# Folding attention's high and low sums by plain turns and a pair sum on VectorE, and a new order of the recurrence's work among the experts

## The reference, cut to what matters

```
x: 4 x 1024 x 512
# layer 0
xn = layernorm(x)
attn: per head h of 8: two score maps softmax(q_i k_i^T, causal), i = 1, 2 (dh 64)
      a = map_1 - map_2 * lambda;  o = a @ v_h           # 1024 x 64 per head
      o = o * rsqrt(mean of squares in groups of 8 + 1e-6) * (1 - l_init);  out = o @ Wo
ffn:  (silu(xn W1) * (xn W3)) -> Hadamard transform -> W2
x = x + attn(xn) + ffn(xn)
# layer 1
xn = layernorm(x)
rec:  f = sigmoid(xn Wf), c = silu(xn Wc), r = silu(xn Wr)
      h_t = f_t h_(t-1) + (1 - f_t) c_t  along the 1024 rows of a batch
      rec = (r * rmsnorm(h)) @ Wo
moe:  router over 64 experts, 8 per token, at most 128 tokens an expert
      expert: (silu(xb Wg) * (xb Wu)) @ Wd, scaled by the gate, added to its tokens
x = x + rec(xn) + moe(xn)
```

## Time and profile before

| what | value |
|---|---|
| median of three runs | 3428.03 us |
| profiled execution | 3419.29 us, span 3417.1 us, clock 0.968 |
| PE busy | 3156.6 us (92%) |
| PEld busy | 2458.4 us (72%) |
| DVE busy | 1780.5 us (52%) |
| ACT busy | 1258.1 us (37%) |
| POOL busy | 1610.9 us (47%) |

### The profile page before, as it was taken

The page is one execution under the profiler, slowest core; times in us unless marked ns, Lnnn a source line. Parts: engine busy times, 40 slices in busy tenths (PEclk is TensorE's granted clock), DMA queues, the critical chain, the costliest instruction groups (busy, mean ns, idle before and its releaser), DMA issues. The chain is left out here.

```text
span 3417.1 us, 45950 instructions
## 1 busy us (share of the span) xinstructions
PE 3156.6 (92%) x16426; PEld 2458.4 (72%) x16426; DVE 1780.5 (52%) x3865; ACT 1258.1 (37%) x2829; POOL 1610.9 (47%) x1410
## 2 busy tenths in 40 slices
PE   5999999899999989999998999999968799998996
PEld 3778787777778777877777787787736567676764
DVE  5455556655555555555566656555536453424431
ACT  3344444434434343443334344333333222332322
POOL 2356657634554653364455336445522334443442
PEclk8999999999999999999999999999979899999998
DMA  7432323353222234211122421112064568685867
GB/s 214 155 117 99 105 90 105 118 176 111 81 90 93 93 114 151 97 65 69 62 81 96 151 98 64 68 62 74 29 218 155 150 169 234 183 221 167 212 182 151
DMA packets 219392, 424.78 MB, mean 124 GB/s; under 512 B 22432, under 2 KB 103072, under 8 KB 217120
## 3 DMA queue, kind: packets, MB, share of 16 engines
q1 hardware_dynamic: 200608, 377.79, 32.9%
q0 software_dynamic: 18560, 44.05, 7.0%
HBM read 311.09 MB, written 110.69 MB: 123 GB/s over the span
## 5 line engine op out<-in xcount | busy, mean ns | idle before, releaser
L776 POOL TENSOR_SCALAR probs<-probs,comb 128x512 f32<-128x512 f32 (+3 forms) x384 | 222.1, 587 | 1017.4 <-DVE comb L725 1017.2
L897 ACT ACTIVATE probs<-score_ps,neg_max 128x640 f32<-128x640 f32 (+7 forms) x512 | 374.8, 739 | 481.5 <-DVE neg_max L731 481.5
L731 DVE TENSOR_REDUCE neg_max<-score_ps 128x2 f32<-128x256 f32 (+7 forms) x256 | 347.3, 1356 | 114.1 <-PE score_ps L1025 113.3
L781 POOL TENSOR_TENSOR probs<-probs 128x512 f32<-128x512 f32 (+3 forms) x384 | 384.5, 1016 | 10.7
L785 POOL TENSOR_TENSOR out_root<-out_root,neg_half 128x16 f32<-128x16 f32 x128 | 372.7, 2912 | 4.8 <-DVE out_root L708 4.8
L820 ACT ACTIVATE attT<-turn_ps 128x512 fp32r<-128x512 f32 (+3 forms) x384 | 189.3, 493 | 470.1 <-PE turn_ps L934 467.9
L633 DVE TENSOR_TENSOR layer_sum<-product_ps,layer_sum 128x512 f32<-128x512 f32 x384 | 262.9, 685 | 30.5 <-PE product_ps L40 24.5
L1022 PE MATMUL score_ps<-keys_all,queries_all 64*128 64x512 f32 (+3 forms) x2304 | 278.0, 364 | 0.0
L620 DVE TENSOR_TENSOR attT<-turn_ps,attT 128x512 fp32r<-128x512 f32 (+3 forms) x384 | 212.8, 554 | 106.8 <-ACT attT L820 104.0
L678 DVE SCALAR_TENSOR_TENSOR hidden<-gate_tanh,product_ps 128x512 f32<-128x512 f32 x128 | 88.1, 688 | 312.8 <-ACT gate_tanh L862 312.8
L1022 PEld LDWEIGHTS score_ps<-keys_all,queries_all 64*128 64x128 f32 x2304 | 187.3, 186 | 67.6 <-issue 31.1
(11 more groups left out here) (280 smaller groups left out, 7297.2 us busy)
## 6 DMA issues: line engine op xcount, KB each, us to landing
w_qk<-weights_split SPq DMA_DIRECT2D x48, 512.0 KB, 4.5
w_gate<-weights_split SPq DMA_DIRECT2D x48, 512.0 KB, 3.3
w_up<-weights_split SPq DMA_DIRECT2D x48, 512.0 KB, 3.6
w_down<-weights_split SPq DMA_DIRECT2D x48, 512.0 KB, 6.5
e_gate_up<-in_w_gate_dram SPq DMA_DIRECT2D x64, 384.0 KB, 3.6
e_gate_up<-in_w_up_dram SPq DMA_DIRECT2D x64, 384.0 KB, 4.7
e_down<-in_w_down_dram SPq DMA_DIRECT2D x64, 384.0 KB, 3.9
values_by_head<-hidden_split SPq DMA_DIRECT2D x32, 512.0 KB, 3.3
```

The lines of the kernel that those rows point to most:

```text
L731: dve.tensor_reduce(nmax[:, i % 2, :], score_tile(i % NT), AX.X, ALU.max, negate=True)\
L776: pool.tensor_scalar(PR[:, r, 1, c], PR[:, r, 1, c], comb[:, i % 4:i % 4 + 1], 1.0, ALU.mult, ALU.mult)\
L781: pool.tensor_tensor(PR[:, r, 0, c], PR[:, r, 0, c], PR[:, r, 1, c], ALU.add).then_inc(s_comb, 1)
L897: act.activation(PR[:, i % 2, q, 0:(j + 1) * P], score_tile(j)[:, q, :], ACT.Exp, bias=nmax[:, i % 2, q:q + 1], accum_out=sums[:, i % 16, ...
```

## The change

In attention, PE no longer multiplies by `fold`. It turns both query tiles of `OT` with the plain 128 x 128 unit matrix into all 256 columns of the upper half of `PV`. A row then holds the 64 high sums and the 64 low sums of a query, and one DVE reduction adds them in pairs, `PV` to `O`, for both tiles. A second DVE instruction, which waits for the first, scales `O` in place by one over the sum of exponentials, both tiles at once. PE's next `values` waits for the reduction; ACT's squares wait for the scaling (a new semaphore, `s_osc`).

In the tail the planner's list and rules change. A turn costs 1.5 in the count, not 0.95. The turns of the next batch, formerly in one row ahead of it, stand between projections: four among the last ones of the batch before, four among the first ones of the batch itself, whose projections now go by half. An expert takes at most 8.2 in the count. `sums` waits for at least two experts from the one in which the squares became due, and in the expert phase a `due` whose scan is not finished is not forced: the expert takes nothing more from the list.

```diff
-                            for q in range(2):
-                                tile = 2 * (g % 4) + q
-                                r = (h * NT + tile) % 16
-                                ins = dve.tensor_scalar(O[:, tile, h % 2 * DH:(h % 2 + 1) * DH],
-                                                        PV[:, 2 * P + q * DH:2 * P + (q + 1) * DH], rsum[:, r, 0:1], None, ALU.mult)
-                            ins.then_inc(s_oxf, 1)
+                            tile = 2 * (g % 4)
+                            r = (h * NT + tile) % 16
+                            o_q = O[:, tile:tile + 2, h % 2 * DH:(h % 2 + 1) * DH]
+                            dve.tensor_reduce(o_q, PV[:, 2 * P:4 * P].rearrange("p (q w n) -> p q n w", q=2, w=2), AX.X, ALU.add)\
+                               .then_inc(s_oxf, 1)
+                            dve.wait_ge(s_oxf, b * GROUPS + g + 1)
+                            dve.tensor_tensor(o_q, o_q, rsum[:, r:r + 2, 0:1].to_broadcast([P, 2, DH]), ALU.mult).then_inc(s_osc, 1)
...
-                        act.wait_ge(s_oxf, b * GROUPS + 4 * (2 * k + 1) + t // 2 + 1)
+                        act.wait_ge(s_osc, b * GROUPS + 4 * (2 * k + 1) + t // 2 + 1)
...
-                                ins = pe.matmul(PV[:, 2 * P + q * DH:2 * P + (q + 1) * DH], OT[:, q * P:(q + 1) * P],
-                                                fold[:, :], start=True, stop=True)
+                                ins = pe.transpose(PV[:, (2 + q) * P:(3 + q) * P], OT[:, q * P:(q + 1) * P], ident[:, :])
...
+            def proj(o, w, c, h):
+                return ("proj", o, w, c, h), 2.7
+
+            def turn(o, t):
+                return ("turn", o, t), 1.5
+
             for o in range(batches + 1):
-                if o and o < batches:
-                    for t in range(NT):
-                        yield ("turn", o, t), 0.95
...
+                elif o < batches:
+                    for w in range(2):
+                        if w:
+                            yield ("due", o - 1, 1), 0
+                        for c in range(2):
+                            yield proj(o, w, c, 0)
+                            yield turn(o, 4 + 2 * w + c)
+                    for w in range(2):
+                        for c in range(2):
+                            yield proj(o, w, c, 1)
...
                     if o:
                         yield ("due", o, 0), 0
-                    for c in range(2, 4):
-                        for h in range(2):
-                            yield ("proj", o, 2, c, h), 2.7
+                    more = o + 1 < batches
+                    yield proj(o, 2, 2, 0)
+                    yield proj(o, 2, 3, 0)
+                    if more:
+                        yield turn(o + 1, 0)
+                    yield proj(o, 2, 2, 1)
...
                     if o == batches - 1:
                         yield ("gap",), 20.0
                         yield ("due", o, 1), 0
...
-                while todo and (e is None or spent + todo[0][1] / 2 <= allowed + busy):
+                while todo and (e is None or spent + todo[0][1] / 2 <= min(allowed + busy, 8.2)):
+                    if todo[0][0][0] == "sums" and s - squared.get(todo[0][0][1:], s) < 2:
+                        break
+                    if todo[0][0][0] == "due" and e is not None and todo[0][0][1:] not in done:
+                        break
```

29 lines of the change are left out of this document (16 added, 13 removed).

## The result

| | before | changed |
|---|---|---|
| median (range), us | 3428.09 (3421.15 to 3428.65) | 3388.81 (3382.12 to 3392.46, 4 runs) |
| profiled execution, us | 3419.29, span 3417.1 | 3390.38, span 3387.2 |
| mean granted clock | 0.968 | 0.964 |

A forecast was written before the change was run, and what follows sets the result against it. Attention was taken as bound by PE, the experts as losing time to stalls and low clock. Attention 12, experts 0 to 51 43, end -4: 51 us gained, 3377 us from the median; 8-in-10 range 3350 to 3412.

The forecast's parts named there:

- The order's 43 us: Experts 0 to 51: stalls and low clock fall from 69 to 26 us, 43 gained, bounds 15 and 57.
- Expert 4's excess: Expert 4: 12.8 us go, since sums now comes two experts or more behind the squares.
- the forced scan: Expert 6's forced scan, paid for by expert 7 (21.8 against 13.2 us), goes: 8.6 us.
- The three rows of turns: Experts 0 to 51: input waits, low parts and low clock at these rows go, 28 us.
- what was to come: New losses in experts 0 to 51: 17 us, with 5.3 in expert 17, 2 in expert 39, 3 unseen.
- The turn's price: Attention, PE: a turn costs 0.11 us, two 0.22 against the fold's 0.38, saving 0.16 a group.
- The rival of a turn that occupies PE for its recorded 0.27: Attention: two turns take 0.54 against 0.38, 20 us lost instead of 12 won; 3409 us, chance 0.05.
- it does not bind: Attention: DVE's extra 0.25 us a group, 32 us, is hidden by its idle time before hidden; 0 to 4 pass on.
- Two signs named for it: Attention: DVE's wait before hidden still there at about 0.5 us; PE's idle time not above 99 us.
- The attention term, -12: Attention: PE's saving of 20.5 us over 128 groups counts in 72 of them, 12 us gained; bounds 0 and 20.5.
- the one that counted 72 of 128 groups: Attention: PE already waited for DVE at 56 of 128 heads_out turns, so only 72 groups gain.
- The end, +4: Expert 52 to the end: sums and eight output tiles behind expert 63, additions setting the pace, 4 us more; -4 to +14.

The follow-up runs named there:

- experiment 4: The kernel with only the new fold, without the scaling by one over the sum of exponentials, against the kernel before: 3423.45 us, ratio 0.9993.
- experiment 5: The kernel with only the new fold, DVE's low part of a turned map moved ahead of the root's product with heads_out: 3405.74 us, 0.9930 to before.
- experiment 3: The changed kernel with the list's entry gap exempt from the limit of 8.2, so sums and output tiles stand in experts 55 to 60: 3379.59 us.

## Why the prediction was right, point by point

**Right: side, place and size.** Faster, inside the range, 12 us above the forecast. The order's 43 us came as 43.4. Its account holds too: of the 44 us by which experts 0 to 51 idled, 17 are left (583.5 - 566.3), and PE's busy time fell by 16.3 as the clock rose from 0.95 to 0.98. Expert 4's excess, the waits for `xn_again` and expert 49's are gone, and so is the forced scan, for which expert 7 paid with a clock of 0.84 (columns as in the earlier trace rows):

```profile
2758.40:2780.20 21.80, 16.09 (x55) 11.05 (x54) 9.38 (x14) 5.09 (x7) 11.64 (x13) 0.84 0.39 112
```

The three rows of turns, to which the prediction gave 28 us, lay in experts 2, 19, 20 and 36. These had 27 us of excess before and have 0.4 in the changed kernel, by the count of the table's "excess". Of what was to come, expert 17 has 5.2 (forecast 5.3) and expert 39 1.8 (forecast 2). I had put 6.4 into experts 4 and 6 to 8, and they have 2.4; expert 5 has 10.2 that I did not see, half of it a wait for POOL's sum of squares, ahead of which the gate products of POOL (7.2 us in one row of seven) stand in its queue. These two errors go opposite ways, 4 us too much and, beyond the 3 allowed for things unseen, 7 too little; so that the sum was met so closely is partly luck.

**The turn's price: right.** 0.54 from the down matmul to the scores, forecast 0.55. The rival of a turn that occupies PE for its recorded 0.27 is refuted: both turns and what follows start within 0.31 us. The same row goes against the reading of the Trainium skill's page "TensorE: Matmul & The Clock Gate", section on PE-mode transpose, as a price per turn. Its 275 ns is the length of one here (mean 276), not the distance between two (0.11).

**DVE: right that it does not bind.** The reduction has 0.415 us (forecast 0.43), the scaling 0.293 at the median and 0.424 at the mean (forecast 0.35), up to 1.195. DVE's busy time grew by 47 us, not 32, and still nothing hung on it, as experiment 4 shows. Two signs named for it came out worse: the wait before `hidden` was found 92 times with 0.72 us each, not at 112, and PE's idle time in attention was 111 us (2360 - 2248.8), above the 99 that it was not to exceed.

**The attention term, -12: mis-sized; measured -5.4, and -7.7 for the fold alone.** (The profile of the new order alone has 3.5 us less in attention than that of before, with the same program there, so both figures may be that much too large.) The failed step is the one that counted 72 of 128 groups and stopped there. The waits took less than it gave them (6.6 us, where 56 groups would be 9.7 by the measured 0.173). What it left out is that PE, arriving earlier at waits of 1.3 us and so waiting 1.46, spends more time at 1.2 GHz: 41.0 against 27.3 us, 6.8 lost, or 11.9 by the other profile. That waits and clock go together is shown by experiment 5, where moving one DVE instruction takes the nine waits and most of the low clock of batches 1 to 3 away. The kernel of experiment 5 has the same turns and no more time at 1.2 GHz in the steps than before (27.3 us), and in batches 1 to 3 it has the same 6.8 us as the old fold with that edit, so the new turns alone don't bring it. The Trainium skill's page "TensorE: Matmul & The Clock Gate" (section on PE-mode transpose) would have it that turns keep the clock up less; experiment 5 speaks against that as the cause here. Why the clock falls at one of two like waits and not at the other is open.

**The end, +4: mis-sized; measured +11.3.** I had followed the additions one behind another and taken PE's experts at 5.0 us each. PE reads rows that the same queue gathers: with nothing but 5 us of work in an expert, a gather behind a chained addition, with 6.4 to 8.2 us to its landing, is late. That the place of `sums` and output tiles is the cause is shown by experiment 3; how much of the lateness is the queue and how much the landing is open. Experts 58 and 60 to 62 have 5.5, 2.0, 1.7 and 2.3 us of excess, and the last half batch was added 101.6 us after expert 52 (3362.71 - 3261.1), not 93.

Two more signs for the tail came out otherwise: the additions came 5.6 to 9.1 us apart from 3295 us on, not 5.7 back to back, and the wait at `sums` for POOL, which was to be gone, is 5.2 us in expert 5 (8.2 in expert 4 before).

**Left out: the stretch ahead of expert 0.** It varies by up to 10 us with the same instructions, so one pair of profiles can't tell a change of that size from none.

## What to carry to other kernels

Where an engine is busy 95% of a stretch, a shorter instruction ahead of a wait is worth less than its own length: count the groups that wait behind it, and then the clock behind each wait. Before giving a fast engine more work, look at the order on the engine that it waits for: an instruction with two SBUF operands that may collide with POOL belongs behind one that reads PSUM, if POOL is free by then, and ahead of it where POOL stays busy (batch 0 of experiment 5 is the one case of that here). A planner's gap or limit must be followed to the queues that feed the emptied experts, not only to those that drain them.

## What the runs showed of the hardware

- DVE instructions with two SBUF operands were held until POOL's instruction ended: 4.57 us for a link of 0.38 beside a product of 4.90, 1.33 us beside four pieces. Of the 128 root products in the kernel with the new fold alone 43 took over 0.6 us, and each ended 0.15 us after an instruction of POOL. The reduction and `hidden`, which read PSUM, never stretched (412 to 416 and 673 to 691 ns in 128 cases each). The page "SBUF — State Buffer" of the Trainium skill (its terms, on the shared port pair) says that DVE and GpSimd take one port pair for a whole instruction and the loser blocks fully; these rows agree. They show besides that splitting POOL's work helps DVE and costs POOL 0.6 us (5.48 for 4.90), and that POOL's product was longer beside DVE as well (4.90 for 4.5 to 4.6 elsewhere).
- In steps 1 to 63 of attention every stretch of PE at 1.2 GHz (113 in fourteen profiles) stood at or just behind a wait of 1.1 to 3.1 us, mostly of 1.2 to 1.6; after some such waits the clock stayed. Experiment 5 took away 5 us of idle time and 13.7 us at 1.2 GHz.
- Two turns of 128 x 128 cost 0.21 us of PE's time together (0.54 - 0.33), though each is recorded with 0.27.
